# Two attention layers on one core: the third set of q rows stored behind the first fill, maxima placed from step 19 on, nine of them moved to the next stage

## The reference, cut to what matters

```python
x = x + _L0_conv_ref(_gn(x), ...)   # global attention, 12 heads of 16, bias by relative row and column
x = x + _L1_conv_ref(_gn(x), ...)   # attention in a 7 x 7 neighbourhood, plus 16 register keys
# layer 0:
attn_bias = (rel_h[:, :, :, :, None] + rel_w[:, :, :, None, :]).reshape(Bx * NUM_HEADS, S, S)
scores = q @ jnp.swapaxes(k, -1, -2) * SCALE + attn_bias
attn = jax.nn.softmax(scores, axis=-1)
# layer 1:
scores = jnp.where(mask_cat[None, None], scores, NEG_INF)
attn = jax.nn.softmax(scores, axis=-1)
```

## Time and profile before

| | us |
|---|---|
| median of three runs | 4865.21 |
| lowest, highest | 4857.58, 4866.6 |
| the profiled execution, its own time | 4862.39 |
| its span in the trace | 4860.6 |

### The profile page before, as it was taken

The page is one execution under the profiler, slowest core; times in us unless marked ns, Lnnn a source line. Parts: engine busy times, 40 slices in busy tenths (PEclk is TensorE's granted clock), DMA queues, the critical chain, the costliest instruction groups (busy, mean ns, idle before and its releaser), DMA issues.

```text
span 4860.6 us, 97545 instructions
## 1 busy us (share of the span) xinstructions
PE 4446.6 (91%) x32598; PEld 2268.6 (47%) x32598; DVE 3079.8 (63%) x5558; ACT 2594.1 (53%) x3955; POOL 892.4 (18%) x1901
## 2 busy tenths in 40 slices
PE   4879999999999999999999999999999999999988
PEld 3334453544535454453544535454453544535434
DVE  3736667666675756657566675756757566675644
ACT  1533556555564655555555565555546555565564
POOL 4122021222202222021222202222031221202111
PEclk7988999999999999999999999999999999999999
DMA  6333152442514433153442424433253432424402
GB/s 123 87 73 77 44 119 64 100 87 56 107 42 107 88 89 75 44 115 68 100 80 58 101 52 103 91 83 75 45 114 75 100 80 49 103 60 100 88 15 40
DMA packets 235869, 386.05 MB, mean 79 GB/s; under 512 B 58396, under 2 KB 133728, under 8 KB 235360
## 3 DMA queue, kind: packets, MB, share of 16 engines
q1 hardware_dynamic: 189280, 266.13, 23.7%
q10 hardware_dynamic: 21504, 75.51, 7.8%
q0 software_dynamic: 24576, 37.80, 4.9%
HBM read 227.79 MB, written 88.08 MB: 65 GB/s over the span
## 4 chain that ended last, share of the span: by engine, by line
PE 71%; DVE 11%; issue 6%; DMA 5%; SPq 5%; ACT 2%; DVEq 0%; ACTq 0%; POOL 0%
PE P L1143 14%; PE P L1161 13%; PE P L1102 12%; DVE mx L909 7%; PE P L966 5%; PE P L967 5%; PE P L1193 4%; PE P L1214 4%; DMA queries<-oraw 4%; PE P L1110 3%; PE P L1079 3%; SPq L514 3%; DVE mxc L915 2%; PE P L1186 1%; PE P L1231 1%
## 5 line engine op out<-in xcount | busy, mean ns | idle before, releaser
L909 DVE TENSOR_REDUCE mx<-P 128x1 f32<-128x512 f32 x3072 | 1921.3, 684 | 457.4 <-PE P L1102 453.3
L779 ACT ACTIVATE probs<-P 128x1024 f32<-128x1024 f32 x1536 | 1507.5, 1022 | 854.0 <-PE P L1161 853.8
L1102 PE MATMUL P<-K,AR 96*128 96x256 f16 x6144 | 1074.1, 278 | 56.6 <-DMA AR<-biases 29.5
L1161 PE MATMUL P<-AR,K 113*128 113x512 f16 x3072 | 924.9, 383 | 13.2 <-DMA AR<-mrow 12.6
L915 DVE TENSOR_REDUCE mxc<-P 128x1 f32<-128x336 f32 (+1 forms) x1536 | 656.3, 474 | 317.9 <-PE P L1111 315.0
L1143 PE MATMUL P<-probs,V 128*17 128x512 f32 x6144 | 813.5, 601 | 5.7 <-ACT probs L779 5.7
L1102 PEld LDWEIGHTS P<-K,AR 96*128 96x128 f16 x6144 | 532.2, 98 | 581.4 <-DVE mx L909 202.0
L795 ACT ACTIVATE probs<-P 128x320 f32<-128x320 f32 (+3 forms) x1632 | 612.1, 437 | 338.2 <-PE P L1214 268.4
L1161 PEld LDWEIGHTS P<-AR,K 113*128 113x128 f16 x3072 | 213.3, 98 | 670.3 <-ACT probs L779 519.6
L1110 PE MATMUL P<-K,A 112*128 112x320 f16 (+1 forms) x1536 | 405.2, 300 | 68.7 <-DVE mx L909 54.9
L1214 PE MATMUL P<-A,K 113*128 113x320 f16 (+2 forms) x1536 | 428.3, 300 | 14.7 <-ACT probs L795 14.3
(11 more groups left out here) (125 smaller groups left out, 3718.4 us busy)
## 6 DMA issues: line engine op xcount, KB each, us to landing
AR<-biases SPq DMA_DIRECT2D x384, 256.0 KB, 7.9
AR<-queries ACTq DMA_DIRECT2D x96, 512.0 KB, 5.9
biases<-xn SPq DMA_DIRECT2D x128, 256.0 KB, 2.6
AR<-queries ACTq DMA_DIRECT2D x96, 256.0 KB, 8.8
K<-oraw POOLq DMA_DIRECT2D x384, 64.0 KB, 4.7
xin<-in_x_dram SPq DMA_DIRECT2D x16, 768.0 KB, 10.5
queries<-oraw SPq DMA_DIRECT2D x384, 32.0 KB, 4.6
QA<-queries SPq DMA_DIRECT2D x192, 64.0 KB, 2.8
```

What stands on the lines that cost most here:

```text
L779: nc.scalar.activation(probs[:, u % RING, j:j + 2, :], P[:, b:b + 2, :], ACT.Exp).then_inc(p_done[0], 1)
L909: V_.reduce_max(mx[:, n // 2, n % 2:n % 2 + 1], bank, AX.X).then_inc(used, 1)
L1102: last = mm(bank[:, QD * (v % 2):QD * (v % 2) + QD], AR[0:ROWS_MAX[0], part % SLOTS, v, c, j, 128 * q:128 * q + 128], K0[0:ROWS_MAX[0], h, ...
L1161: last = mm(P[:, j, :], K0[0:ROWS, h, 128 * kt:128 * kt + 128], AR[0:ROWS, p % SLOTS, kt // 2, :, j, :], start=True, stop=True)
```

## The change

`plan_l1`, with a next image: the maxima of phases 0 and 1 were 66 jobs from step 25 to the end less three. Now they are the 33 of phase 0 and the first 24 of phase 1, from step 19 on. The other nine of phase 1 (maxima 24 to 31 and the transpose) stand ahead of phase 2's 33 in the next `plan_l0`, evenly over 22 steps, where 33 stood over 20. Image 0 keeps its own plan. The stage of bare jobs that makes the maxima of image 1, ahead of the loop, loses the same nine. On SP the third set's q rows (`query_rows_out(im, 2)`) are stored behind fill 0 and no longer in prep0. On ACT the wait for them goes from `rows_moved` into `late_rows_moved`, ahead of the result copies of the second set of heads on.

```diff
-THIRD = 16
+THIRD, SECOND = 16, 24
...
-        placed = evenly(max_jobs(0, image, 2), 0, 20)
+        placed = evenly(max_jobs(0, image, 1)[SECOND:] + max_jobs(0, image, 2), 0, 22)
...
-    placed += evenly(max_jobs(0, n0, 0) + max_jobs(0, n0, 1), 25, STEPS[1] - TAIL)
+    placed += evenly(max_jobs(0, n0, 0) + max_jobs(0, n0, 1)[:SECOND], 19, STEPS[1] - TAIL)
...
-        yield "jobs", 0, n0, first_phases(n0, *max_jobs(0, n0, 1), *stat_jobs(1, i0))
+        yield "jobs", 0, n0, first_phases(n0, *max_jobs(0, n0, 1)[:SECOND], *stat_jobs(1, i0))
...
-                for g in range(G):
+                for g in range(G - 1):
...
-                    for s, (t, ready) in enumerate(((HI, hi_done), (LO, lo_done))):
-                        sp.wait_ge(ready[0], im * G + g + 1)
-                        for j in range(GH):
-                            sp.dma_start(queries[g, s, :, :, j, :],
-                                         t[D * j:D * j + D, g, :].rearrange("d (a n) -> d a n", a=4)
-                                         ).then_inc(queries_out[g], 16)
+                    query_rows_out(im, g)
                 query_blocks(im, 1)
+
+            def query_rows_out(im, g):
+
+                for s, (t, ready) in enumerate(((HI, hi_done), (LO, lo_done))):
+                    sp.wait_ge(ready[0], im * G + g + 1)
+                    for j in range(GH):
+                        sp.dma_start(queries[g, s, :, :, j, :],
+                                     t[D * j:D * j + D, g, :].rearrange("d (a n) -> d a n", a=4)
+                                     ).then_inc(queries_out[g], 16)
...
                     fill_slot(image, part)
+                    if part == 0:
+                        query_rows_out(image, 2)
...
-            prepared = []
+            prepared, late = [], []
+
+            def late_rows_moved():
+
+                while late:
+                    act.wait_ge(queries_out[2], (late.pop() + 1) * PER_QUERIES)
...
-                    for g in range(G if pl == 0 else 0):
+                    for g in range(G - 1 if pl == 0 else 0):
                         act.wait_ge(queries_out[g], (pi + 1) * PER_QUERIES)
+                    if pl == 0:
+                        late.append(pi)
...
                     rows_moved()
+                    late_rows_moved()
...
                 rows_moved()
+                if g:
+                    late_rows_moved()
```

## The result

| | before | after |
|---|---|---|
| median, us | 4864.91 | 4910.13 |
| lowest, highest | 4857.58, 4866.6 | 4904.52, 4917.53 |
| span of the profiled execution | 4860.6 | 4912.3 |

The ratio after to before is 1.0091, 95% interval 1.0075 to 1.0108: 45 us slower, where 60 us faster was forecast, and outside the range.

What follows compares the result with a forecast made beforehand. Main1 was taken to end on DVE's rate, main0 mostly on PE. 14 main1 gain 126 us, 15 main0 cost 72, the bare maxima save 6.5: net 60.5 less, 4805 us from 4865.2; range 4760 to 4862.

Steps and rivals of the forecast that it cites:

- Main1's gain, 9.0 us: Each of 14 main1: 10.6 us of waits for DVE mostly go and PE issues less; 9.0 us gained, bounds 6 to 11.5.
- The early start, cost 0.5: Main1 steps 19 to 24: added maxima make step 25 1.6 us later, of which 1.1 comes back; cost 0.5.
- wait for the fill of over 1 us: Main1 step 19, whose maximum needs slot 0: a longer wait would show the forecast wrong; 0.3 us was expected.
- Main0's cost, 4.8: Each of 15 main0 takes nine more jobs and gets 4.8 us longer, bounds 2.0 to 6.5.
- SP's stores, nothing: SP's queue: storing the third set behind the first fill gains and costs nothing; bounds zero to 18 us gained.
- The stage of bare maxima, -6.5: Ahead of the loop, the stage for image 1 ends nine jobs earlier, 6.5 us less.
- The third set in the way: Rival: its stores on SP did delay the QA load, or main1's waits all vanish; 4740 to 4770 us, chance 0.12.
- PE is the bound: Rival, no change: PE then waits for ACT's exponentials and a main1 gains 5, not 9; 4861 us, chance 0.14.
- the sign for ACT: Main1's chain: ACT at more than 3 us there would show the forecast wrong.
- The slower one: Rival: added jobs in main0's steps 13 to 21 stall attention, a main0 costs 10.4 us; 4889 us, chance 0.12.

Runs made afterwards that it cites:

- the move alone: Kernel before, with nine jobs moved from main1 to main0, main1's 57 still from step 25, stores in their old place: 4876.70 us, ratio 1.0022.
- PE's half of the columns alone: Kernel before, with scores of main1's 66 maxima computed for half of the keys only, DVE still reducing full rows: 4840.40 us, ratio 0.9941.

## Why the prediction was wrong, point by point

- **Main1's gain, 9.0 us.** This term failed. Its waits were read rightly, and the maxima's part left the chain (5.3 of the 10.6 us). The step from them to time was wrong: 10.6 us of chain were counted as time to be had back, without the work that ran beside them. The earlier trace rows showed it, PE busy for 46.5 of 49 us beside DVE's 40.9. Even with DVE's load gone the piece from store to store gives 3.7 us (main1 with 16 scores per maximum). The change gives 1.5; the same move with the start at 25 gives 3.2. Relief of DVE alone brings no more than that, where 9.0 us were forecast. (Of the 66 jobs 64 are maxima, so DVE's need was 39 us and not the 40 of the prediction; nothing hangs on it.)
- **The early start, cost 0.5.** It costs 1.3 to 2.3 us a round with 57 jobs. The forecast had step 25 come 1.6 us later, and L1113 behind step 24 came 1.3 (mean) to 2.0 us later, so this was right. The 1.1 us that were to come back in the steps behind did not. The "wait for the fill of over 1 us" was named as a sign; it was 0.9 in the round shown, and the chain there goes on to layer-1 maxima on DVE.
- **Main0's cost, 4.8.** Right at +4.8 as a sum, and in part by luck: steps 0 to 12 cost 1.4 us where 1.1 was forecast, steps 13 to 19 1.2 in place of 2.6, steps 20 and 21 1.6 in place of 1.1, and 0.5 arises ahead of the first scores, where nothing was forecast.
- **SP's stores, nothing.** Right in the loop, where the wait for QA stayed (2.6 us a round, 2.5 before, as means). Wrong ahead of it, by 6 to 9 us: the queue was followed through one round and not through the first image, where the constant rows stand behind. (An issue takes 0.68 us there, 5.4 for eight, and 0.70 in the earlier trace rows, not the 0.6 of the prediction.)
- **The stage of bare maxima, -6.5.** The first round holds it and one main0, -1.7 by the forecast, -1.6 measured. Only this sum was seen, and it varies: with the move alone the first round was 3.8 us shorter than before.
- **The clock** was no term. It took 10 to 20 us.
- **The rivals.** The third set in the way: refuted, as read. "PE is the bound", given 0.14, had the right place, but named ACT for the wait, which holds 0.8% of the chain with DVE relieved, and PE is not the bound alone; the sign for ACT, over 3 us of main1's chain, did not come (ACT's two lines in it are 4.3% of 49 us, 2.1). The slower one was nearest in time (4889), but its cause, a main0 longer by 8.8 or more, did not come. The page of the Trainium skill that spoke for "PE is the bound" (Perfetto Trace Analysis, Identifying the Most-Contended Engine: work on the engine of the highest occupancy first, with the warning that matmul busy time misleads) was set aside because the chain disagreed with it. The runs side with it for one half: PE at 91% was no average to be read away, and with PE's half of the columns alone the gain is still 1.6 us, since DVE is level with it.

The sum by measured parts: stores 6 to 7, the move 7 to 12, the start at 19 on top of the move some 32, together 45 to 51 against 45. The clock's 10 to 20 us are contained in these parts; which part holds how much was not separated.

## What to carry to other kernels

A wait in the chain is worth what is left when the other engine's work in its shadow has been done: read the other engine's busy time in the same stretch first, and if a doubt stays, price the wait by shortening the work that causes it, before anything is moved. Where two engines are level, work taken off one pays little (2.8 and 1.6 us here, against 7.9 for both), and work moved to the next stage has to be paid there (4.8 us). Follow a moved DMA through the first iteration as well, where nothing hides its issue.

## What the runs showed of the hardware

A plan that only spread 16 small maxima over later steps cost 0.85%, and 42 of its 45 us go with the granted clock (143 us more of half clock, at 0.29; not tested in that kernel): it went to half in main1's head and stayed at 0.50 while PE was busy for 4.00 of 4.00 us in three stretches in a row (1514 to 1526 us, above). Twenty products of 1.8 us in all, whose results nobody reads, earned 9 us back in one kernel and 20 in another, though they stood ten us ahead of the wait that seemed the cause, and filling that wait earned nothing that could be measured.
